# Token rows gathered by a computed list in the q, k and v products, in place of rows scattered and read back

## What is computed

```python
def _fff(x, nw, nb, w1, b1, w2, b2, act):      # NN = 255 nodes, NL = 256 leaves, LW = 16
    node = jnp.zeros(x.shape[:2], dtype=jnp.int32)
    for _ in range(DEPTH):                     # DEPTH = 8
        logit = jnp.einsum('bsd,bsd->bs', x, nw[node]) + nb[node]
        node = 2 * node + 1 + (logit > 0).astype(jnp.int32)
    leaf = node - NN
    h = act(jnp.einsum('bsd,bsdl->bsl', x, w1[leaf]) + b1[leaf])
    return jnp.einsum('bsl,bsld->bsd', h, w2[leaf]) + b2[leaf]

xn = (x - mu) / jnp.sqrt(sd + 1e-05)
q, k, v = (_fff(xn, ..., relu) for each of three trees)
att = softmax(einsum('bqd,bkd->bqk', q, k) / sqrt(D))
y = xn + einsum('bqk,bkd->bqd', att, v)
return y + _fff(y, f_nw, ..., gelu)
```

## Time and profile before

| what | us |
|---|---|
| timed executions | 1450.51, 1457.71, 1457.75 |
| their median | 1457.71 |
| span of the profiled execution | 1547.4 |
| TensorE matmuls busy in it | 1243.8 (80%) |
| VectorE busy | 872.7 (56%) |
| ScalarE busy | 548.2 (35%) |
| GpSimd busy | 445.7 (29%) |
| routing, q, k, v tables in it | 93, 114, 68, 65 |

### The profile page before, as it was taken

How to read it: one execution, slowest core, us unless ns; L and a number is a source line. 1 busy time by engine, 2 the same in 40 slices (tenths; PEclk the granted TensorE clock), 3 DMA queues, 4 the chain that set the end, 5 groups by cost and what they waited for, 6 DMA issues and landing times. The chain is left out here.

```text
span 1547.4 us, 24565 instructions
## 1 busy us (share of the span) xinstructions
PE 1243.8 (80%) x7200; PEld 909.5 (59%) x7204; DVE 872.7 (56%) x2484; ACT 548.2 (35%) x1074; POOL 445.7 (29%) x587
## 2 busy tenths in 40 slices
PE   2297999998957673578875856869999979999998
PEld 1185777776746562466654745646666645555554
DVE  8998899999134542346452553634565533454444
ACT  1134566665222131346542314513434331212120
POOL 2267344544450437131216417131121000000000
PEclk9558999999879876799987977877999989999999
DMA  9000000000006322667434625250010000000000
GB/s 266 0 2 1 1 2 1 1 1 1 1 9 182 117 84 100 199 205 234 154 95 152 197 73 121 72 142 8 8 15 8 2 1 1 14 0 14 0 14 14
DMA packets 90117, 97.06 MB, mean 63 GB/s; under 512 B 20041, under 2 KB 74827, under 8 KB 89997
## 3 DMA queue, kind: packets, MB, share of 16 engines
q1 hardware_dynamic: 77708, 70.32, 15.0%
q0 software_dynamic: 12288, 25.26, 6.3%
HBM read 76.59 MB, written 18.96 MB: 62 GB/s over the span
## 5 line engine op out<-in xcount | busy, mean ns | idle before, releaser
L2170 PE MATMUL gq_psH<-gq_xT,gq_w 128*128 (+1 forms) x564 | 103.2, 310 | 46.3 <-ACT gq_act L1903 26.4
L2170 PEld LDWEIGHTS gq_psH<-gq_xT,gq_w 128*128 128x128 f32 x564 | 83.3, 210 | 72.2 <-issue 68.1
L2180 PE MATMUL gq_psY<-leaf_w,gq_hT 128*128 (+1 forms) x282 | 94.1, 418 | 15.1 <-DVE gq_hT L2056 10.2
L2843 DVE TENSOR_REDUCE c_max<-c_psA 128x8 f32<-128x2048 f32 x32 | 73.4, 2294 | 54.9 <-PE c_psA L2993 54.9
L3319 ACT ACTIVATE m_silu<-m_psG 128x512 f32<-128x512 f32 x48 | 28.7, 597 | 213.5 <-PE m_psU L3439 213.5
L3372 DVE TENSOR_TENSOR m_act<-m_silu,m_psU 128x512 f32<-128x512 f32 x48 | 33.0, 688 | 120.7 <-ACT m_silu L3319 106.0
L2075 DVE TENSOR_TENSOR gq_y<-gq_psY,gq_y 128x256 f32 (+1 forms) x141 | 59.6, 423 | 71.5 <-remote 47.0
L3439 PE MATMUL m_psG<-m_xnT,m_gate 128*128 128x512 f32 x192 | 90.7, 594 | 2.1 <-PEq L193 2.1
L3439 PE MATMUL m_psU<-m_xnT,m_up 128*128 128x512 f32 x192 | 90.2, 592 | 0.0
L1785 POOL DMA_INDIRECT gq_y<-in_group_b,gq_row_leaf x48 | 46.0, 958 | 141.4 <-DVE gq_row_leaf L2047 131.8
L2751 ACT ACTIVATE c_probT<-c_psA 128x2048 f32<-128x2048 f32 x32 | 60.1, 1877 | 62.7 <-PE c_psA L3027 62.7
(11 more groups left out here) (527 smaller groups left out, 3020.6 us busy)
## 6 DMA issues: line engine op xcount, KB each, us to landing
leaf_w<-in_group_w SPq DMA_DIRECT2D x128, 128.0 KB, 3.5
leaf_w<-in_group_w SPq DMA_DIRECT2D x64, 256.0 KB, 4.7
gq_x<-sorted_x_v SPq DMA_DIRECT2D x16, 130.0 KB
gq_x<-sorted_x_k SPq DMA_DIRECT2D x16, 129.5 KB
gq_x<-sorted_x_q SPq DMA_DIRECT2D x16, 129.0 KB
rows_f<-token_rows SPq DMA_DIRECT2D x8, 257.0 KB
a_w<-in_L_xattn_W SPq DMA_DIRECT2D x2, 1024.0 KB, 13.1
sorted_y_q<-gq_y SPq DMA_DIRECT2D x16, 128.0 KB, 3.9
```

Of the source, the lines that this page charges most:

```text
L2170: last = pe.matmul(psH[n % 2][:, 0:P], w1[n % 3][:, c, :], xT[:, c, bass.ds(g * -P + u * P, P)], start=(c == 0), stop=(c == DC - 1))
L2180: pe.matmul(psY[n % 3][:, 0:D], hT[n % 2][:], weights.w2[:, bass.ds(g * D, D)], start=True, stop=True).then_inc(y_ps, 1)
L2843: dve.tensor_reduce(out[:, :, :, SUM_ROW], psA[:], AX_X, ALU.max).then_inc(maxes.s, 1)
```

## The change

The rows in token order are stored once, by SyncE, to `rows_x` (8 stores of 256 rows, between q's weight loads). The scatters, the tensors `sorted_x_q/k/v`, the reads back and the step `token` are gone. In their place `locate`, `find_tokens` and a new `found_tokens` work for all three tables: TensorE adds up the token numbers and leaves of the sorted rows, and GpSimd gathers each sorted tile from `rows_x` into the ring itself. Rows of `xs` are D wide; the leaf comes from the new `sorted_leaf`. The pieces of the ranking get other places among routing items and among the units of q. In the last product `locate` has one more product, reading back has five operations, and a row is D wide.

```diff
+    def store(self, sp, b):
+        sp.wait_ge(self.norm, b + 1)
+        sp.dma_start(self.core.rows_x[b * S:(b + 1) * S, :].rearrange("(t p) d -> p t d", p=P),
+                     self.rows[:, b * ST:(b + 1) * ST, 0:D]).then_inc(self.rows_out, 16)
...
-                def place(f):
-                    pool.wait_ge(slots_in, f + 1)
-                    if route:
-                        pool.wait_ge(route.norm, B)
-                        pool.wait_ge(route.G_sb, (f + 1) * B)
-                    for t in range(NT):
-                        pool.indirect_dma_start(
-                            core.sorted_x[first + f],
-                            bass.IndirectOffsetOnAxis(core.back[:, f, t:t + 1], 0),
-                            rows[:, t, 0:width(first + f)], None).then_inc(placed[f], 16)
+                def gather(f, t):
+                    n = f * NT + t
+                    if t == 0:
+                        pool.wait_ge(found_in, f + 1)
+                    if n >= RING:
+                        pool.wait_ge(x_ps, n - RING + 1)
+                    pool.indirect_dma_start(
+                        xs[n % RING][:], None, core.rows_x if route else core.rows_f,
+                        bass.IndirectOffsetOnAxis(token_i[:, f, t:t + 1], 0)
+                        ).then_inc(tile_in[n % RING], 16)
...
                 if route:
                     route.pool(pool)
-                    place(0)
-                    pool.wait_ge(route.G_sb, route.ITEMS)
-                    for t in range(NT):
-                        seed(0, t)
-                    for f in range(1, nf):
-                        place(f)
-                    for f in range(1, nf):
-                        for t in range(NT):
+                    pool.wait_ge(route.rows_out, 16 * B)
+                    for f in range(nf):
+                        for t in range(RING):
+                            gather(f, t)
+                        if f == 0:
+                            pool.wait_ge(route.G_sb, route.ITEMS)
+                        for t in range(RING):
+                            seed(f, t)
+                        for t in range(RING, NT):
+                            gather(f, t)
                             seed(f, t)
...
                     for j in range(PAIRS8):
                         weights.load_pair(sp, first, j)
-                    for t in range(RING):
-                        tile(0, t)
+                        if j % 2:
+                            route.store(sp, j // 2)
...
+                def found_tokens(f):
+                    dve.wait_ge(found_ps, f + 1)
+                    found = psZ[:, 0:3 * NT].rearrange("p (k t) -> p k t", k=3)
+                    do.mark(dve.tensor_copy(sorted_leaf[:, f], found[:, 2]))
+                    do(dve.tensor_copy(tile_row[:, 0], found[:, 0]))
+                    do.mark(dve.tensor_tensor(token_i[:, f], tile_row[:, 0], found[:, 1], ALU.add))
+                    do.mark(dve.tensor_tensor(
+                        leaf_row[:, f], sorted_leaf[:, f],
+                        leaves.offset[:, first + f:first + f + 1].to_broadcast([P, NT]), ALU.add))
+                    do.wait()
+                    dve.tensor_copy(tile_row[:, 1, 0:1], tile_row[:, 0, 0:1]).then_inc(found_in, 1)
...
                 def store(b):
                     sp.wait_ge(y_sb, b + 1)
-                    sp.wait_ge(g_sb, b + 1)
```

More of the change, by code:

```diff
@@ L1586, in dve_take @@
                 last.then_inc(self.routed, 1)
[L1588 to L1594, removed]
     def pe_turn(self, pe, b):
@@ L2015, in number_tokens, with locate @@
                                          None, ALU.subtract))
[L2017 removed]
+                def locate(f, k):
                     tile, place = tile_row[:, 0], tile_row[:, 1]
[L2019 to L2039 removed]
@@ L2041, in token @@
-                def token(f, t):
-                    if nf == 1:
-                        return
-                    n = f * NT + t
-                    dve.wait_ge(tile_in[n % RING], 16 * (n // RING + 1))
-                    at = leaf_at(first + f)
-                    dve.tensor_tensor(leaf_row[:, f, t:t + 1], xs[n % RING][:, at:at + 1],
-                                      leaves.offset[:, first + f:first + f + 1], ALU.add
-                                      ).then_inc(token_in, 1)
+                    if k == 0:
+                        do(dve.tensor_scalar(tile, slot[:, f, :], -HALF_K, 1.0 / P, ALU.add,
+                                             ALU.mult))
+                        do(dve.tensor_scalar(tile, tile, ROUND, ROUND, ALU.add, ALU.subtract))
+                        do.mark(dve.scalar_tensor_tensor(place, tile, -float(P), slot[:, f, :],
+                                                         ALU.mult, ALU.add))
+                        do(dve.tensor_tensor(is_tile[:],
+                                             tile.unsqueeze(2).to_broadcast([P, NT, NT]),
+                                             column[:, 0:NT].unsqueeze(1).to_broadcast([P, NT, NT]),
+                                             ALU.is_equal))
+                        for n, value in enumerate((tile_no[:], rows[:, :, leaf_at(first + f)])):
+                            do.mark(dve.tensor_tensor(
+                                ids[:, :, 2 * n], is_tile[:],
+                                value.unsqueeze(2).to_broadcast([P, NT, NT]), ALU.mult))
+                        do(dve.tensor_scalar(ids[:, :, 1], is_tile[:], leaves.row_no[:, 0:1], None,
+                                             ALU.mult))
+                    else:
+                        half = NT // 2
+                        for n in range(2):
+                            q = slice(n * half, (n + 1) * half)
+                            dve.tensor_tensor(is_row[:, q],
+                                              place[:, q].unsqueeze(2).to_broadcast([P, half, P]),
+                                              column[:].unsqueeze(1).to_broadcast([P, half, P]),
+                                              ALU.is_equal).then_inc(numbered, 1)
@@ L2120, in _ @@
                         slots(0, k)
-                    locate()
+                    for k in range(2):
+                        locate(0, k)
+                    found_tokens(0)
                     for k in range(2):
@@ L2127, in _ @@
                     clear(0, t)
-                for t in range(AHEAD):
-                    token(0, t)
                 g = next_group(dve, found, 0, 0, 0)
```

209 lines of the change are left out of this document (86 added, 123 removed).

## The result

| | before | changed |
|---|---|---|
| timed median, us (11 executions each) | 1452.00 | 1459.59 |
| ratio, 95% interval | | 1.0046 (1.0028 to 1.0065) |
| span of the profiled execution | 1547.4 | 1456.6 |
| forecast | | 1462, range 1424 to 1478 |

The change costs half a per cent.

What follows compares the result with a forecast made beforehand. It took all engines to halt during trains of indirect DMAs, mostly absent from timed runs, with no engine near full. Without halts, +11 + 3 + 5 - 15 - 1 + 1 = +4 us on 1457.7 gave 1462, range 1424 to 1478.

Steps and rivals of the forecast that it cites:

- The likeliest case: Whole kernel: the sum worked without halts, 1450 to 1469 us, given a chance of 0.44.
- q's first 16 units: Start of q table: GpSimd's 26 gathers and seeds after the routing set the pace, +11 us (6 to 14).
- VectorE in the routing: Routing: new numbering of sorted rows exceeds VectorE's slack, +3 us.
- VectorE in q: q table, units 15 to 20: v's numbering and reading back exceed VectorE's slack, +5 us.
- SyncE's queue before k: k's tile loads no longer queue behind weights and stores, -15 us (-5 to -22); T is TensorE's first q turn.
- v: v table: the 3.80 us wait for v's tile goes, GpSimd's pace costs 2.5, net -1 us.
- attention, last product: Last product stage: one more product and four short operations before the first gather, 16 matmuls fewer, +1 us.
- The choice between the clocks: Profile span 1547.4 against timed 1457.7 us: most halts taken as missing in timed runs, so sum worked without them.
- The halts are real: Rival, chance 0.30: all engines halt during indirect DMA trains in timed runs too; about -31 us, 1427 (range 1405 to 1449).
- GpSimd becomes the bound: Rival, chance 0.26: k's tiles wait under about 7 us in SyncE's queue, so pairs' cost prevails; +20, 1478 us.
- the pair's pace: q, k and v tables: GpSimd issues gather and seed in turn at 2.5 us a pair.
- tile 6 as the first to wait: q table: TensorE's transposes wait for gathers from tile 6 on, behind the six early gathers.

Runs made afterwards that it cites:

- e5: The changed kernel unchanged, run again in a session without halts: 1458.73 us against 1454.56 for the kernel before, ratio 1.0037 (1.0019 to 1.0055).
- e6: The kernel before, unchanged, profiled in a session without halts: span 1450.7 us.
- e12: The changed kernel with GpSimd's q seeds waiting only for the routing's last logits, session without halts: 1452.15 us against 1456.58, ratio 0.9984.
- e9: The kernel before with ten pairs of k's weights and six of v's, not three, ahead of tile loads awaiting scatters: 1446.45 us against 1457.34, ratio 0.9946.
- e11: The changed kernel with all 16 seeds of k and of v ahead of the ten later gathers, session without halts: 1448.43 us, ratio 0.9934.
- e10: The changed kernel with v's ranking pieces at units 6 to 16 of q, not 9 to 24, session without halts: 1453.77 us, ratio 0.9980.
- e1: The kernel before, unchanged, profiled a second time, in a halting session: span 1552.6 us, timed executions between 1541 and 1557 us.
- e2: The changed kernel with all k and v seeds ahead of the ten later gathers, in a halting session: 1533.65 us, ratio to before 0.9901.
- e3: The changed kernel with v's ranking pieces at units 6 to 16 of q, in a halting session: 1535.35 us, ratio to before 0.9920.
- e4: The changed kernel with q's seeds waiting only for the routing's last logits, in a halting session: 1529.07 us, ratio to before 0.9877.
- e7: The changed kernel with the edits of e2, e3 and e4 together and a ring of 10 buffers, not 6: 1435.02 us, ratio to before 0.9876.

## Why the prediction was right, step by step

The sum was +4 us; the profiles of one session give +5.6, the timings 4.2 and 7.6. The likeliest case (1450 to 1469) held: without halts, q loses to GpSimd's count and to VectorE's pieces, and k wins by SyncE's queue. Its terms:

| step | forecast | measured (e5 less e6) | |
|---|---|---|---|
| q's first 16 units | +11 | +9.7 | 33.5 against 23.8; price and mechanism right (e12) |
| VectorE in the routing | +3 | +0.6 | +3.0 to +3.5 by the six other profiles without halts |
| VectorE in q | +5 | +9.9 | mis-sized |
| SyncE's queue before k | -15 | -9.9 | mechanism right (e6, e9), sizes off |
| v | -1 | -3.7 | its wait is 6.80 us, not 3.80; its pairs cost 4.8, not 2.5 (e11) |
| attention, last product | +1 | -1.0 | |

The sum is nearer than its terms, and that is in part luck: two of them came out 10 us dearer together, the other four 8.4 us cheaper. That 1462 lies only 2.4 us from 1459.6 is luck too: it starts from 1457.7, the median of three executions, where that of eleven is 1452.0.

*VectorE in q.* The forecast priced only operations against slack. TensorE's clock was left out: busy time grew by 5.4 us (39.14 against 33.76) at a granted clock of 0.86 instead of 0.96 (28% and 8% of the time at the lower of its two levels). Fourteen more matmuls, all short, make 1.1 of it (34.82 in e10, at 0.96), the clock 4.3. Waits alone grew by 4.5 us, about the 5 forecast.

*The queue.* The forecast had the tile landing at T + 76 and TensorE there at T + 58; e6 has T + 85 (626.23) and, with the wait of 12.29 taken off, T + 73. Both were early. The rest of q takes 38.7 us for 31 units, 1.25 us each, not the 0.98 read from two units of the earlier trace rows. The wait is 12.3 us, not 18, and the net gain 9.9. The difference, 2.4 us, isn't the price of the pairs: by e11 they take 6.6 us of k's table. Without them k needs 53.0 us, 16.5 less than before, since with the wait gone TensorE is also busy for less time (52.05 us at a clock of 1.00, for 54.47 at 0.88). So -18 + 2.5 in the forecast stands against -16.5 + 6.6: the pairs were mis-sized most.

*v.* The row at 748.11 isn't the first turn of v, as its heading says, but that of tile 6, and it is from a halting profile.

*The choice between the clocks.* "Most of the halts are missing in the timed runs" held for the runs that counted. The sentence that they would then "belong to the profiled execution alone" was wrong (e1). The gap of 89.7 us is that between the two kinds of session.

*The rivals.* "The halts are real" is true of a halting session, but its 31 us (2.1%) are not. The same three kernels have these ratios without halts and with them: e11 and e2 0.9934 and 0.9901, e10 and e3 0.9980 and 0.9920, e12 and e4 0.9984 and 0.9877. So a halting session adds 0.3 to 1.1% to the gain; for the changed kernel with its 1.0037 that would be an estimate of 0.993 to 1.000, and no run shows it. Routing and q gain much as forecast (8.5 and 24.4 us in e4, for 6 and 31), but the forecast let k and v go free, and they lose time (79.2 and 70.3 us). "GpSimd becomes the bound" decides at a wait of 7 us; it was 12.3. In q's turns GpSimd did become the bound, as the sum had it, and e7 shows what its order and VectorE's pieces together were worth: 24 us.

Right as forecast, too: the pair's pace, tile 6 as the first to wait, a q table of 83 us with a timed gain near nothing.

## What to carry to other kernels

Where work moves from a queue with slack (SyncE) to one that counts (GpSimd at 1.25 us an indirect DMA), look at the order inside it: here the place and start of GpSimd's seeds were worth 17.6 us of the tables (e11, e12) and the place of VectorE's pieces 7.3 (e10), where the change itself cost 4 to 8. A wait hidden in a DMA queue (12.3 us for k's tile 6) is found by adding up what stands in front of it, and here two numbers took half of it away (e9). If the span of a profile is far from the timed runs, take a second profile before arguing from the first: here stages with the same instructions differed by 9.5 us between profiles even without halts.

## What was not expected of the hardware

- The same program takes about 1455 us in one session and 1550 us in another, on the same chip; in profiles of the two kinds the four stages in which trains of indirect DMAs run account for the whole surplus (102.9 us, for 101.9 in the span). In the worst stretch TensorE, VectorE and ScalarE are busy 0.0, 0.25 and 0.32 of 14 us.
- Short waits cost twice: in the rest of q, where TensorE waited 0.4 to 1.9 us behind VectorE's pieces, the granted clock was 0.86 and 215 matmuls took 39.1 us; in e10, with most of those waits gone, it was 0.96 and they took 34.8.
